# Latent attention on one Trainium2 core: the narrow product with each head's rows gathered, run as two 64-column products in the halves of the array

## The reference

```python
y = layernorm(x)                                  # 16 x 128 x 256
q = y @ Wq[h].T @ w_kc_q[h]                       # per head: 128 rows of 192 numbers
q = q * cos + concat(-q[96:], q[:96]) * sin       # rotary, halves of 96
q = q @ W_qr[h]                                   # 192 -> 64   (then w_kc_kv, W_kr on the keys' side)
p = softmax(q @ rotated_context.T)                # 128 x 128 per head and sequence
x = x + concat_h(p @ rotated_context ...) @ Wo
```

## Time and profile before

| what | us |
|---|---|
| median of 3 runs | 924.28 |
| the profiled execution itself | 926.4 |
| its span, first to last instruction | 924.8 |
| PE busy | 811.0 (88%) |
| VectorE busy | 667.6 (72%) |
| GpSimd busy | 502.7 (54%) |
| ScalarE busy | 395.6 (43%) |
| mean granted TensorE clock | 0.946 |

### The profile page before, as it was taken

How to read it: one execution, slowest core, us unless ns; L and a number is a source line. 1 busy time by engine, 2 the same in 40 slices (tenths; PEclk the granted TensorE clock), 3 DMA queues, 4 the chain that set the end, 5 groups by cost and what they waited for, 6 DMA issues and landing times. The chain is left out here.

```text
span 924.8 us, 15048 instructions
## 1 busy us (share of the span) xinstructions
PE 811.0 (88%) x4785; PEld 568.8 (61%) x4792; DVE 667.6 (72%) x1203; ACT 395.6 (43%) x1056; POOL 502.7 (54%) x495
## 2 busy tenths in 40 slices
PE   3999999679989898579999999999999979766775
PEld 2554544347767677456777777776777659653443
DVE  4898987468887878647666666666666725998894
ACT  2687877322222222123444444444444363213442
POOL 3555555216665656505555555555555549535774
PEclk9999999779999999959999999999999979888999
DMA  9100000040000000030101101010000000000001
GB/s 270 59 1 0 0 1 1 0 151 18 18 17 18 17 17 0 9 117 12 46 1 46 38 11 46 0 45 0 1 1 1 1 1 2 0 0 1 29 29 35
DMA packets 8755, 24.54 MB, mean 27 GB/s; under 512 B 1711, under 2 KB 4143, under 8 KB 8087
## 3 DMA queue, kind: packets, MB, share of 16 engines
q1 hardware_dynamic: 8154, 23.81, 7.7%
q10 hardware_dynamic: 549, 0.08, 0.1%
HBM read 21.79 MB, written 2.10 MB: 26 GB/s over the span
## 5 line engine op out<-in xcount | busy, mean ns | idle before, releaser
L1122 PE MATMUL ps<-yt_all,a 128*128 128x512 f32 x576 | 140.9, 398 | 0.0
L1284 POOL TENSOR_TENSOR p<-p,l_inverse 128x512 f32<-128x512 f32 x64 | 66.5, 1039 | 125.9 <-DVE l_inverse L1247 125.9
L1122 PEld LDWEIGHTS ps<-yt_all,a 128*128 128x128 f32 x576 | 106.4, 189 | 26.2 <-issue 5.0
L773 PE MATMUL ps<-yt_experts,wsplit 128*128 (+1 forms) x384 | 102.5, 419 | 10.0 <-DVE h L867 8.3
L1202 ACT ACTIVATE p<-ps,l_negmax 128x128 f32<-128x128 f32 x256 | 89.8, 377 | 37.3 <-DVE l_negmax L1254 37.3
L1254 DVE TENSOR_REDUCE l_negmax<-ps 128x4 f32<-128x512 f32 x64 | 41.3, 687 | 81.9 <-PE ps L1165 81.9
L1233 DVE TENSOR_TENSOR turned<-ps,rope 128x1024 f32<-128x1024 f32 x64 | 78.3, 1224 | 29.3 <-PE ps L1122 25.5
L394 DVE TENSOR_REDUCE negmax<-ps 128x4 f32<-128x512 f32 x128 | 85.4, 688 | 11.5 <-PE ps L243 9.6
L773 PEld LDWEIGHTS ps<-yt_experts,wsplit 128*128 128x128 f32 x384 | 75.0, 202 | 28.3 <-DVE inner L861 7.6
L1142 PE MATMUL ps<-q,b 128*128 128x512 f32 x192 | 88.5, 597 | 1.0 <-issue 1.0
L325 ACT ACTIVATE pt<-ps 128x512 f32<-128x512 f32 x128 | 72.8, 596 | 8.3 <-PE ps L263 4.1
(11 more groups left out here) (185 smaller groups left out, 1662.3 us busy)
## 6 DMA issues: line engine op xcount, KB each, us to landing
wide<-in_wide SPq DMA_DIRECT2D x8, 768.0 KB, 4.2
mx_raw<-in_mx SPq DMA_DIRECT2D x8, 384.0 KB, 3.1
x<-in_x SPq DMA_DIRECT2D x4, 512.0 KB, 8.7
ctx_t<-in_ctx_t SPq DMA_DIRECT2D x1, 2048.0 KB, 7.8
narrow<-in_narrow SPq DMA_DIRECT2D x8, 256.0 KB, 4.5
out<-x SPq DMA_DIRECT2D x16, 128.0 KB, 1.7
ktraw<-in_ctx_rows SPq DMA_DIRECT2D x1, 1248.0 KB
wraw<-in_gate SPq DMA_DIRECT2D x1, 1024.0 KB, 18.2
```

The lines of the kernel that those rows point to most:

```text
L773: t = pe.matmul(out, w_at(pw, w + k * EXPERTS * INTER + x * INTER, INTER), run_of(m.yt[:, py, k, :, :], j).rearrange("p b s -> p (b s)"), ...
L1122: t = pe.matmul(tile_ps[k], a[par][:, pa, kin, k * 128:(k + 1) * 128], m.yt[:, py, kin, 4 * j:4 * j + 4, :].rearrange("p b s -> p (b s)"), ...
L1284: pool.tensor_tensor(p[:, head, :, :], p[:, head, :, :], spread(inverse[:, head, :], 2, S), ALU.mult).then_inc(normed[head], 1)
```

## The change

The first 64 of each half of a head's 192 numbers now lie in tile 0 (first half) and tile 1 (second half), with head 0 in rows 0 to 63 and head 1 in rows 64 to 127; what is left of both heads lies in tile 2. The rotary sum of tile 1 is moved to the other half of the partitions, so that for each head 128 rows of `q` stand together. The first part of the narrow product is then one product for each head, 128 rows by 64 columns, whose outputs are the upper and the lower half of one bank; the second part is one product of 128x128 from tile 2, as before. `q` of tiles 0 and 1 gets two buffers. POOL makes the unmoved sums (two of 64x512, `q0_made`) and the sum of tile 2 (`q2_made`), VectorE makes the moved sums (two of 64x512, `q1_made`), at the end of its step. The copy of the context product goes from VectorE to ScalarE, ahead of the exponentials. The third rotary product of tile 2 comes before the reciprocal for head B on VectorE. Pieces 0 and 1 have four products instead of three, piece 3 has two instead of three. The host lays out the weights and tables to match.

```diff
@@ PE: the narrow product
-                    pe.wait_ge(q01_made, n)
+                    pe.wait_ge(q0_made, n)
+                    pe.wait_ge(q1_made, n)
+                    wait(pe, qs_made, n - 1)
+                    for head in range(2):
+                        pe.matmul(q_ps[rows[head], :], b[weights][:, 0, head * CE:(head + 1) * CE],
+                                  q[(j - 1) % 2][:, head, :], start=True, stop=False)
                     pe.wait_ge(q2_made, n)
-                    wait(pe, qs_made, n - 1)
-                    for k in range(TILES):
-                        t = pe.matmul(q_ps, b[weights][:, k, :], q[:, k, :], start=(k == 0), stop=(k == TILES - 1))
-                    t.then_inc(narrowed, 1)
+                    pe.matmul(q_ps, b[weights][:, 1, :], q2[:, :], start=False, stop=True).then_inc(narrowed, 1)
@@ ACT: at the head of its step
+                if inside(n - 3, STEPS):
+                    act.wait_ge(ctx_made, n - 2)
+                    act.activation(m.ctxt[:, i if j >= 3 else i - 1, (j - 3) % GROUPS * N:((j - 3) % GROUPS + 1) * N],
+                                   ctx_ps, ACT.Copy).then_inc(ctx_kept, 1)
@@ DVE: its step
-                if inside(n - 3, STEPS):
-                    dve.wait_ge(ctx_made, n - 2)
-                    dve.tensor_copy(m.ctxt[:, i if j >= 3 else i - 1, (j - 3) % GROUPS * N:((j - 3) % GROUPS + 1) * N],
-                                    ctx_ps).then_inc(ctx_kept, 1)
...
                     rotate(4, 2, 4)
                     rotate(5, 2, 5, slice(CE, 2 * CE), slice(0, CE))
+                    rotate(5, 2, 5, slice(0, CE), slice(CE, 2 * CE)).then_inc(tile_turned[2], 1)
                 invert(n, 1)
+                extra()
                 if inside(n, STEPS):
-                    rotate(5, 2, 5, slice(0, CE), slice(CE, 2 * CE)).then_inc(tile_turned[2], 1)
-                extra()
+                    wait(dve, narrowed, n - 1)
+                    dve.wait_ge(tile_turned[0], n + 1)
+                    dve.wait_ge(tile_turned[1], n + 1)
+                    for head in range(2):
+                        t = dve.tensor_tensor(q[j % 2][rows[1 - head], head, :], turned[rows[head], 1, :],
+                                              turned[rows[head], 3, :], ALU.add)
+                    t.then_inc(q1_made, 1)
@@ POOL: after the two products p
+                    wait(pool, narrowed, n - 1)
+                    wait(pool, normed[1], n - 1)
+                    wait(pool, q2_made, n)
+                    for head in range(2):
+                        t = pool.tensor_tensor(q[j % 2][rows[head], head, :], turned[rows[head], 0, :],
+                                               turned[rows[head], 2, :], ALU.add)
+                    t.then_inc(q0_made, 1)
+                    pool.wait_ge(q0_made, n + 1)
+                    pool.wait_ge(tile_turned[2], n + 1)
                     wait(pool, narrowed, n)
-                    pool.tensor_tensor(q[:, 0, :], turned[:, 0, :], turned[:, 2, :], ALU.add)
-                    pool.tensor_tensor(q[:, 1, :], turned[:, 1, :], turned[:, 3, :], ALU.add).then_inc(q01_made, 1)
-                    pool.wait_ge(tile_turned[2], n + 1)
-                    pool.tensor_tensor(q[:, 2, :], turned[:, 4, :], turned[:, 5, :], ALU.add).then_inc(q2_made, 1)
+                    pool.tensor_tensor(q2[:, :], turned[:, 4, :], turned[:, 5, :], ALU.add).then_inc(q2_made, 1)
@@ PE, pieces 0 and 1 (piece 3: range(TILES) becomes range(2))
-                        both = w_ps[:, 0:256].rearrange("p (t c) -> p t c", t=2)
-                        cut = slice(0, CQH) if head == 0 else slice(CQH, 128)
-                        width = 2 * CQH if head == 0 else 2 * (128 - CQH)
-                        t = pe.matmul(both[:, :, cut], wq,
-                                      wide[:, head, E:E + width].rearrange("p (t c) -> p t c", t=2), start=True, stop=True)
-                    t = pe.matmul(w_ps[:, 256:384], wq, wide[:, 1, E + width:E + CQ], start=True, stop=True)
+                        both = w_ps[:, 0:256].rearrange("p (t h c) -> p t h c", t=2, h=2)[:, :, head, :]
+                        rest = w_ps[:, 256:384].rearrange("p (t h c) -> p t h c", t=2, h=2)[:, :, head, :]
+                        for out, columns in ((both, wide[:, head, E:E + 128]), (rest, wide[:, head, E + 128:E + CQ])):
+                            t = pe.matmul(out, wq, columns.rearrange("p (t c) -> p t c", t=2), start=True, stop=True)
```

More of the change, by code:

```diff
@@ L47 @@
 HEADS, CQ, CQH, KDIM = 16, 192, 96, 128
-THIRD = 128 - CQH
 FFN, MX = 1024, 32
@@ L1032, in latent_attention @@
         a = [sb(f"a{i}", [128, 2, HALVES, TILES * 128], F32R) for i in range(2)]
-        b = [sb(f"b{i}", [128, TILES, 2 * CE]) for i in range(2)]
+        b = [sb(f"b{i}", [128, 2, 2 * CE]) for i in range(2)]
         turned = sb("turned", [128, 2 * TILES, N])
-        q = sb("q", [128, TILES, N])
+        q, q2 = [sb(f"q{i}", [128, 2, N]) for i in range(2)], sb("q2", [128, N])
         qs = sb("qs", [2 * CE, N])
@@ L1045, in latent_attention @@
         tile_made, tile_turned = [sem(f"l_tile{t}") for t in range(TILES)], [sem(f"l_turned{t}") for t in range(TILES)]
-        q01_made, q2_made, narrowed, qs_made = sem("l_q01_made"), sem("l_q2_made"), sem("l_narrowed"), sem("l_qs_made")
+        q0_made, q1_made, q2_made = sem("l_q0_made"), sem("l_q1_made"), sem("l_q2_made")
+        narrowed, qs_made = sem("l_narrowed"), sem("l_qs_made")
         scored, max_made, exp_made, inverted, normed, p_turned, p_kept = (
@@ L1112, in prepare @@
                     pe.wait_ge(c_lo, i + 1)
-                    for k in range(TILES):
+                    for k in range(2):
                         t = pe.matmul(w_ps[:, k * 2 * CE:(k + 1) * 2 * CE], narrow[:, k * 128:(k + 1) * 128],
-                                      narrow[:, TILES * 128:], start=True, stop=True)
+                                      narrow[:, 2 * 128:], start=True, stop=True)
                     t.then_inc(b_made, 1)
@@ L1262, in step @@
                         dve.wait_ge(tile_made[k], n + 1)
-                        wait(dve, q01_made, n)
+                        wait(dve, q0_made, n)
+                        wait(dve, q1_made, n)
                         rotate_both(k).then_inc(tile_turned[k], 1)
@@ L1706, in program @@
             m.wide = [sb(f"wide{i}", [KDIM, 2, E + CQ + CE + E]) for i in range(2)]
-            m.narrow = [sb(f"narrow{i}", [2 * CE, 4 * 128]) for i in range(2)]
+            m.narrow = [sb(f"narrow{i}", [2 * CE, 3 * 128]) for i in range(2)]
             def first_heads(sp):
@@ L1735, in shape_constants @@
     sin, cos = sin.T, cos.T
-    third, rest = slice(0, THIRD), slice(THIRD, CQH)
-    first_tiles = [np.concatenate([v, v[third]]) for v in (cos[:CQH], sin[CQH:], -sin[:CQH], cos[CQH:])]
-    last_tile = [np.concatenate([cos[:CQH][rest], cos[CQH:][rest]]), np.concatenate([sin[CQH:][rest], -sin[:CQH][rest]])]
+    most, rest = slice(0, 64), slice(64, CQH)
+    first_tiles = [np.concatenate([v[most], v[most]]) for v in (cos[:CQH], sin[CQH:], -sin[:CQH], cos[CQH:])]
+    last_tile = [np.concatenate([v[rest], v[rest], w[rest], w[rest]])
+                 for v, w in ((cos[:CQH], cos[CQH:]), (sin[CQH:], -sin[:CQH]))]
     rope = np.stack(first_tiles + last_tile, axis=1)
@@ L1777, in laid_out @@
     wo = grouped(heads("Wo"), 0).reshape(E, HEADS, KDIM).transpose(1, 2, 0)
[L1778 to L1782, removed]
+    wkq, wqr = heads("w_kc_q"), heads("W_qr").transpose(0, 2, 1)
+    order = np.concatenate([np.arange(64), CQH + np.arange(64), np.arange(64, CQH), CQH + np.arange(64, CQH)])
+    wkq, wqr = wkq[:, :, order], wqr[:, :, order]
     wide = np.concatenate([wq, wkq, heads("w_kc_kv"), wo], axis=2)
     d["wide"] = wide.reshape(HEADS // 2, 2, KDIM, -1).transpose(0, 2, 1, 3)
[L1786 to L1790, removed]
+    narrow = np.zeros((HEADS // 2, 2, CE, 3 * 128), np.float32)
+    narrow[:, 0, :, 0:128] = wqr[0::2][:, :, 0:128]
+    narrow[:, 1, :, 0:64], narrow[:, 1, :, 64:128] = wqr[1::2][:, :, 64:128], wqr[1::2][:, :, 0:64]
+    for head in range(2):
+        for half in range(2):
+            c = 128 + half * 64 + head * 32
+            narrow[:, head, :, c:c + 32] = wqr[head::2][:, :, 128 + half * 32:160 + half * 32]
     wkr = heads("W_kr").transpose(0, 2, 1)
-    narrow[:, 0, :, 384:384 + CE], narrow[:, 1, :, 384 + CE:] = wkr[0::2], wkr[1::2]
-    d["narrow"] = narrow.reshape(HEADS // 2, 2 * CE, 4 * 128)
+    narrow[:, 0, :, 256:256 + CE], narrow[:, 1, :, 256 + CE:] = wkr[0::2], wkr[1::2]
+    d["narrow"] = narrow.reshape(HEADS // 2, 2 * CE, 3 * 128)
     t = ctx.transpose(2, 0, 1)
```

2 lines of the change are left out of this document (1 added, 1 removed).

## The result

The changed kernel takes 939.19 us (936.1 to 940.96, 4 runs) beside 924.42 for the kernel before on the same chip. The ratio is 1.0153, 95% interval 1.0122 to 1.0184. It is slower, by 14.8 us where 9 had been forecast: inside the wide range of 925.5 to 941 and outside the forecast's own 930 to 936. The profiled execution has a span of 938.5, 13.6 more than before (the spans are taken before rounding).

The account below looks back on a forecast made before the run. PE was taken as the bound, with POOL's product close behind. Terms -0.8, +4.0, +4.8, -0.7 and +1.7 gave +9.0, 935.4 profiled, 933 us on the median; own range 930 to 936, eight in ten 925.5 to 941.

Parts of the forecast that it names:

- PE saves 0.66 a step: Narrow product on PE: two 64-column products side by side cost 0.86 plus 0.20 for shape changes, saving 0.66 us a step.
- The chain to POOL, step 10.60: Head B's reciprocal on VectorE starts 0.70 later, POOL's product ends at T + 7.81, PE waits, step takes 10.60 us.
- The collision, 0.50 in 11 steps, steps of 11.10: Piece-3 steps and last pair: VectorE's first moved sum goes ahead of POOL's product, making it 0.50 us late.
- Rival (a): Both moved sums on VectorE go ahead of POOL's product: 11 steps by 0.65, +7.2, 940.5 us; chance 0.16.
- (b): The collision of moved sums with POOL costs nothing, the sum starting after POOL's product: -5.5, 928 us; chance 0.14.
- (c): The pair of narrow products on PE does not run side by side: 19 steps cost 0.25 more, 938 us; chance 0.07.
- (e): The forecast chain from tile 2 to POOL's end is 0.3 a step too long: -9, 924.3 us, even; chance 0.10.
- (d): The wait for POOL does not bind, PE's 0.66 is gained in 30 steps: 904 us, or half, 914; chance 0.07.
- The copy on ScalarE, +1.7 at the end: Context copy delays the exponentials by 0.9 in each of two steps after the last, less 0.1: +1.7 us.
- Step 1, which waits for no POOL product, -0.7: Term for step 1 in the sum: no POOL product is waited for there, so it gains 0.7 us.
- wait, which nobody needs: Steps with pieces 0 to 2: POOL's product starts first, VectorE's moved sums wait, `q1` being wanted 4.4 us into the next step.

Follow-up runs that it names:

- experiment 8: Changed kernel with both reciprocals before tile 2's products, POOL's tile 2 sum waiting for the moved sums in steps 0 and 1, context copy on VectorE after step 31: 908.48 us.
- experiment 1: Changed kernel with VectorE's reciprocal for head B put back before the third rotary product of tile 2: 914.54 us, ratio 0.9900.
- experiment 2: Changed kernel with one wait added, VectorE's moved sums waiting until POOL's product for head B is done: 933.13 us, ratio 1.0093.
- experiment 4: Kernel before with the reordering alone, the third rotary product of tile 2 ahead of the reciprocal for head B: 929.25 us, ratio 1.0063.
- experiment 3: Changed kernel with the first moved sum directly behind the reciprocal for head B in every step, ahead of VectorE's part of the piece: 948.90 us, ratio 1.0282.
- experiment 7: Changed kernel with both reciprocals before the products of tile 2: 913.99 us, ratio 0.9884.

## Why the prediction was right, and where it was short

- **PE saves 0.66 a step: right.** 2.58 became 1.97, so 0.61; the pair took 1.01 for the 0.86 and a change of shape that were reckoned. In whole steps, with POOL out of the way (experiment 8), it is 0.60 on the mean of steps 3 to 30, from 0.43 to 0.84.
- **The chain to POOL, step 10.60: right.** 10.60 outside the loops, 10.66 to 10.71 in most steps of the loop body; experiments 1, 2 and 4 show the cause. That it came out to the hundredth is in part luck. POOL's product ended at T + 7.84 (forecast 7.81), head B's transposes followed 0.05 later (0.15), and from them to the next T it was 2.71 (2.64). The 0.07 more in the loop body (steps 8 to 23) is nearly all in the second of these: with pieces 0 to 2 the transposes follow 0.13 after POOL there. Why is open.
- **The collision, 0.50 in 11 steps, steps of 11.10: right.** 1.54 for 1.04, steps of 11.10 to 11.14. Experiment 2 takes it away, experiment 3 makes more of it.
- **Rival (a), both sums ahead of POOL, is out.** The second sum let POOL in; its product would have been 2.2. The time of 939 lies near (a)'s 940.5 for another reason. Rivals (b), (c) and (e) are out too (1.54; four passes in 1.01; no step of the changed kernel from step 2 on under 10.59), and (d) is what experiments 7 and 8 make true.
- **The copy on ScalarE, +1.7 at the end: right**, 1.5. One reading behind it does not add up: 733.33 and 0.60 give 733.93, not 733.75. In step 31 the exponentials began 0.62 after T (744.29) where they had begun 0.19 ahead of it, so 0.8 late.
- **The step that failed is the first steps.** The sum said: "Step 1, which waits for no POOL product, -0.7", and counted step 2 as any other; of the blocked sums it said that they "wait, which nobody needs". In steps 0 and 1 PE runs 6.0 and 9.05 apart and VectorE is what is behind (it makes step 0's sums 2.1 us into step 1), and two sums at 2.4 instead of 1.39 make it later. In step 2 that lateness reached POOL's products and so PE. Steps 0 and 1 gave 0.3 together and not 0.7 (step 1, with piece 1, gave 0.43, which is what such a step gives at PE's own length), and step 2 cost 3.6.

The account of the 13.6 us of span: before the stage -0.8, steps 0 and 1 -0.3, step 2 +3.6, steps 3 to 27 +4.4 (269.72 against 265.33), last pair +5.0, end +1.5, behind the stage +0.3. The forecast had -0.7, 0, +3.2, +4.8 and +1.7 for the middle five. So 3.6 of the missing 4.6 is step 2 and 1.2 nearly all the hundredths of the loop body; the others about cancel.

## What to carry to other kernels

When the bound engine gets shorter, look first at which instruction of another engine it meets next and how much margin is left there; here it was 0.1 to 0.8 us, and a 0.69 us instruction moved ahead of the one that releases it cost as much as the whole saving (16.8 us from step 3 to step 31 between experiments 1 and 2; the saving there is 16.7). A sum of two SBUF tensors on VectorE beside a GpSimd instruction was paid here by the one that came second (POOL's product 1.54 for 1.04, or the two sums 2.72 for 1.39), so put it where the second one is not waited for. Judge the first and the last steps of a skewed loop by themselves, since there the cover differs.

## What the runs showed of the hardware that was not expected

The prediction had foreseen, from one pair of rows, that two VectorE sums issued back to back don't hold GpSimd off together, and the runs bear it out: in the 11 steps where the first sum started 0.05 us ahead, POOL's product took 1.54 (0.50 more, one sum of 0.69), and in the step shown the two sums took 2.13 instead of 1.39. GpSimd got in between them in every one of these steps.

Two things were not expected. TensorE's granted clock fell in one step and not in others with waits as long: 0.88 in step 2 of the changed kernel, with waits of 0.96 and 1.53 us, and 1.00 in its last pair, with waits of 1.51. And the pair starts later than the product that it replaces: in the last pair, where it follows the tiles directly, at T + 4.32 (experiment 8) for T + 4.22 (the kernel before). So the saving there is 0.61 from the pair's start to the transposes and only 0.48 to 0.49 in the step.
